# Feed-forward weights stored as they are and turned by the DMA that loads them, in a one-core attention and feed-forward block

## What is computed

```python
def block_qdq_weight(w, block=32, bits=4):
    wb = w.reshape(out_f, in_f // block, block)
    qmax = 2 ** (bits - 1) - 1
    scale = jnp.maximum(jnp.max(jnp.abs(wb), axis=-1, keepdims=True) / qmax, 1e-12)
    wq = jnp.clip(jnp.round(wb / scale), -qmax - 1, qmax) * scale
...
x = x + attention(layernorm(x), ctx, Wq, Wk, Wv, Wo)      # x: 8 x 128 x 512
h = act_qdq(layernorm(x))
up, gate = act_qdq(h @ wu.T), act_qdq(h @ wg.T)           # w_gate, w_up: 1376 x 512
gate = act_qdq(gate * fixed_qdq(sigmoid(gate)))
x = x + act_qdq(gate * up) @ wd.T                         # w_down: 512 x 1376
```

## Time and profile before

| | us |
|---|---|
| median of 3 runs | 944.35 |
| lowest, highest | 943.86, 945.84 |
| span of the profiled execution | 944.5 |
| attention groups, first L363 to the last project matmul | 110.6 to 695.6 |
| gate and up matmuls (L465) | 711.9 to 827.8 |
| last matmuls (L515) | 884.2 to 941.2 |

### The profile page before, as it was taken

How to read it: one execution, slowest core, us unless ns; L and a number is a source line. 1 busy time by engine, 2 the same in 40 slices (tenths; PEclk the granted TensorE clock), 3 DMA queues, 4 the chain that set the end, 5 groups by cost and what they waited for, 6 DMA issues and landing times. The chain is left out here.

```text
span 944.5 us, 16272 instructions
## 1 busy us (share of the span) xinstructions
PE 861.5 (91%) x5390; PEld 539.1 (57%) x5390; DVE 663.7 (70%) x1333; ACT 452.6 (48%) x1029; POOL 256.4 (27%) x382
## 2 busy tenths in 40 slices
PE   9999999999899999989999999999868999900898
PEld 3444777767577776657766677767533444400343
DVE  5754588886478888558888656667647459989741
ACT  5344455645346554436554454454513029868630
POOL 0000245453235464224455322222210002203000
PEclk9999999999989999999999999999998999965799
DMA  8013022222012313002232620000030000000001
GB/s 289 1 56 111 20 84 90 90 68 90 3 57 80 111 45 112 23 25 77 92 101 75 210 74 1 2 1 1 1 123 1 1 0 1 1 0 0 12 33 45
DMA packets 39756, 52.14 MB, mean 55 GB/s; under 512 B 2432, under 2 KB 18816, under 8 KB 39680
## 3 DMA queue, kind: packets, MB, share of 16 engines
q1 hardware_dynamic: 39680, 51.13, 16.7%
HBM read 40.37 MB, written 10.75 MB: 54 GB/s over the span
## 5 line engine op out<-in xcount | busy, mean ns | idle before, releaser
L523 ACT ACTIVATE arena<-bank 128x512 f16<-128x512 f32 (+1 forms) x329 | 189.5, 599 | 342.8 <-PE bank L363 234.9
L698 DVE SCALAR_TENSOR_TENSOR arena<-bank,arena 128x512 f16<-128x512 f32 (+1 forms) x329 | 219.1, 686 | 87.8 <-ACT arena L523 87.7
L270 PE MATMUL bank<-arena 128*128 128x256 f16 (+2 forms) x1872 | 261.8, 292 | 0.0
L270 PEld LDWEIGHTS bank<-arena 128*128 128x128 f16 (+1 forms) x1872 | 183.8, 98 | 69.0
L1067 POOL TENSOR_SCALAR arena<-arena,rsum 128x256 f32<-128x256 f32 x256 | 135.2, 528 | 241.2 <-DVE rsum L792 223.5
L465 PE MATMUL bank<-arena 128*128 128x512 f16 x528 | 116.3, 384 | 8.9 <-DVE arena L698 8.9
L387 PE MATMUL bank<-arena 128*128 (+1 forms) x512 | 121.0, 379 | 0.7 <-ACT arena L523 0.7
L579 ACT ACTIVATE arena<-bank,nmax 128x256 f32<-128x256 f32 x256 | 118.1, 487 | 6.2 <-DVE nmax L788 6.2
L784 DVE TENSOR_REDUCE nraw<-bank 128x2 f32<-128x512 f32 x128 | 85.4, 689 | 36.1 <-PE bank L352 36.1
L352 PE MATMUL bank<-arena 128*128 (+1 forms) x768 | 97.4, 277 | 9.4 <-issue 7.2
L352 PEld LDWEIGHTS bank<-arena 128*128 128x128 f16 x768 | 75.8, 99 | 33.6 <-issue 11.2
(11 more groups left out here) (91 smaller groups left out, 738.9 us busy)
## 6 DMA issues: line engine op xcount, KB each, us to landing
arena<-in_w_units SPq DMA_DIRECT2D x33, 256.0 KB, 2.8
w_ready<-arena SPq DMA_DIRECT2D x33, 256.0 KB, 2.1
arena<-w_ready SPq DMA_DIRECT2D x3, 2816.0 KB, 10.9
arena<-in_wq SPq DMA_DIRECT2D x32, 256.0 KB, 2.9
arena<-in_wo SPq DMA_DIRECT2D x32, 256.0 KB, 2.7
arena<-in_x SPq DMA_DIRECT2D x1, 2048.0 KB, 15.4
out<-arena SPq DMA_DIRECT2D x8, 256.0 KB, 2.0
arena<-in_wk SPq DMA_DIRECT2D x4, 256.0 KB, 5.2
```

The lines of the kernel that those rows point to most:

```text
L270: last = nc.tensor.matmul(bank, a(i, c), b(j, c), start=start and c == 0 and n == 0, stop=stop and c == chunks - 1 and n == 2)
L523: return nc.scalar.activation(dst, src, ACT.Copy, scale=scale)
L698: return nc.vector.scalar_tensor_tensor(out=dst, in0=src, scalar=scale, in1=part, op0=ALU.mult, op1=ALU.subtract)
```

## The change

PE's transposes of the weight units are gone, with their semaphore `w_mm`. ACT and DVE split a unit straight from `f_w`, so `w_ready` holds it untransposed. The slot of `f_w` is now free when `unit_lo` has read it (`w_lo`). SP's three loads become 33 transposing DMAs, one for each unit: 22 at the place of the first two, 11 at the place of the third.

```diff
             sp.wait_ge(pv_mm, 2 * QUADS + 1)
-            wgu_flat = wgu.rearrange("p u r n -> p u (r n)")
-            sp.dma_start(wgu_flat[:, 0:FT], ready_d[:, 0:FT]).then_inc(wg_loaded, 16)
-            sp.dma_start(wgu_flat[:, FT:2 * FT], ready_d[:, FT:2 * FT]).then_inc(wu_loaded, 16)
+            def load_turned(dst, u, loaded):
+                sp.dma_start_transpose(dst.rearrange("p r (c n) -> p (r c) n", n=P), w_ready[u]).then_inc(loaded, 16)
+            for u in range(FT):
+                load_turned(wgu[:, u], u, wg_loaded)
+            for u in range(FT, 2 * FT):
+                load_turned(wgu[:, u], u, wu_loaded)
             sp.wait_ge(wo_mm, NG * QUADS + 1)
-            sp.dma_start(wd_s.rearrange("p u r n -> p u (r n)"), ready_d[:, 2 * FT:UNITS]).then_inc(wd_loaded, 16)
+            for u in range(FT):
+                load_turned(wd_s[:, u], 2 * FT + u, wd_loaded)
...
-            def transpose_w(g, k):
-                v = g * FT + k
-                pe.wait_ge(w_dq, v + 2)
-                pe.wait_ge(w_lo, v + 1)
-                for c in range(HC):
-                    mm = nc.tensor.transpose(banks[WB][:, c * P:(c + 1) * P], f_w[:, k % 2, c * P:(c + 1) * P], ident[:, :])
-                mm.then_inc(w_mm, 1)
...
-                if not last(g) and 1 <= k <= FT:
-                    transpose_w(g, k - 1)
...
-            pe.wait_ge(wg_loaded, 16)
+            pe.wait_ge(wg_loaded, 16 * FT)
...
-                act.wait_ge(w_mm, v + 2)
+                act.wait_ge(w_dq, v + 2)
...
-                hi(f_out[:, k % 2, 0], banks[WB][:, :], W_SCALE).then_inc(w_hi, 1)
+                hi(f_out[:, k % 2, 0], f_w[:, k % 2], W_SCALE).then_inc(w_hi, 1)
...
-                lo(f_out[:, k % 2, 1], banks[WB][:, :], f_out[:, k % 2, 0], W_SCALE).then_inc(w_lo, 1)
+                lo(f_out[:, k % 2, 1], f_w[:, k % 2], f_out[:, k % 2, 0], W_SCALE).then_inc(w_lo, 1)
...
-                pool.wait_ge(w_mm, v + 1 if k == 0 else v)
+                pool.wait_ge(w_lo, v + 1 if k == 0 else v)
```

More of the change, by code:

```diff
@@ L161, in build @@
         q_mm, q_hi, q_lo = sem("q_mm"), sem("q_hi"), sem("q_lo")
-        amax_out, wscale_fl, wscale_out, w_norm, w_clip, w_round, w_dq, w_mm, w_hi, w_lo = (
-            sem(n) for n in ("amax_out", "wscale_fl", "wscale_out", "w_norm", "w_clip", "w_round", "w_dq", "w_mm", "w_hi", "w_lo"))
+        amax_out, wscale_fl, wscale_out, w_norm, w_clip, w_round, w_dq, w_hi, w_lo = (
+            sem(n) for n in ("amax_out", "wscale_fl", "wscale_out", "w_norm", "w_clip", "w_round", "w_dq", "w_hi", "w_lo"))
         ln2_stat, ln2_mv, ln2_var, ln2_rstd, ln2_out = (sem(n) for n in ("ln2_stat", "ln2_mv", "ln2_var", "ln2_rstd", "ln2_out"))
@@ L300, in _ @@
             keep_warm(8)
-            for s in (wo_mm, w_mm):
-                pe.sem_inc(s, 1)
+            pe.sem_inc(wo_mm, 1)
             pe.wait_ge(kv_free, NG)
@@ L493, in _ @@
             ffn_tiles(0, 1, 1, g_mm, g_free)
-            pe.wait_ge(wu_loaded, 16)
+            pe.wait_ge(wu_loaded, 16 * FT)
             for t in range(4):
@@ L503, in _ @@
             keep_warm(16)
-            pe.wait_ge(wd_loaded, 16)
+            pe.wait_ge(wd_loaded, 16 * FT)
             pe.wait_ge(u_free, 2 * FT + 3)
```

## The result

| | before | after |
|---|---|---|
| median (lowest to highest), us | 944.35 (942.13 to 945.84), 5 runs | 951.73 (950.29 to 954.43), 5 runs |
| ratio after to before, 95% interval | | 1.0077 [1.0051, 1.0104] |
| span of the profiled execution, us | 944.5 | 948.5 |
| start of the last attention step, us | 686.3 | 693.4 |
| first matmul of the feed-forward part | 711.9 | 716.3 |

The change makes the kernel 0.8% slower. The forecast was slower by 2.0 us; it is 7.4. The profiled execution of after is the fastest of its five: 950.29 with a span of 948.5, so 1.8 us lie around the span. With the same 1.8 us around it, that of before (944.5) would stand at 946.3 (an estimate), some 2 above its median here. That is why the spans are only 4.0 us apart.

What follows compares the result with a forecast made beforehand. PE sets the pace now, and DVE was to replace it at the same pace. A group -0.44 + 0.7 + 0.4 = +0.66, three groups +2.0: 946.5, median 0.15 lower, so 946.3 us; forecast 943 to 949.5, range 938 to 956.

Steps and rivals of the forecast that it cites:

- the hidden loads: 33 transposing loads before the feed-forward part: between 1.0 and 5.8 us a unit, both hidden, so no cost.
- the second rival: Attention steps: unit_lo and the last split both lose their turn to POOL in every step; 950 to 956 us, chance 0.15.
- steps 1: Step 1 of each group, where no split is due before: the full gain, -0.44 us a group.
- steps 2 to 8: Seven attention steps of each group: between 0 and +0.9 us, taken as +0.7 a group.
- steps 9 to 11: End of each group, where the next unit is late behind step 9's query weight splits: taken as +0.4 us a group.
- behind the attention: The program's tail, from 711.9 us on: no change.
- that late step: Second step of a pair: exponentials start late, unit_lo goes first (0.68 us), L1081 waits 0.5, last split precedes L1087 (0.92).
- The replay: Step 3 replayed from profile rows with turns between DVE and POOL, then a whole group: +0.66 us a group.
- The rival's price: Both splits losing every turn: another 0.4 us a step in seven steps and 0.4 behind them; +3.5 a group, +10.5 in all.
- the alternation of the forecast: Steps 2 to 9: two kinds in turn, some 8.7 and some 9.3 to 9.7 us; a pair 18.3, against 18.25 now.
- Rival 1: Attention: PE stays the bound, DVE fits, pairs take 17.4 to 17.9 us; 932 to 942 us, chance 0.21.

Runs made afterwards that it cites:

- The two halves of the change: Kernel before with only its three loads replaced by the transposing ones, 944.28 us; changed kernel with the three plain loads put back, 954.8 us.
- the moved operand: Changed kernel with unit_lo reading a PSUM bank instead of f_w: 930.22 us, ratio 0.9835.
- after_pool_late: Changed kernel with one tiny POOL multiplication added just ahead of unit_normalise (L1076): 947.77 us, ratio 1.0028.
- late_split: Changed kernel with the low part of unit k-2 split in step k, just ahead of the block scales, where POOL is idle: 927.48 us, ratio 0.9808.

## Why the prediction was right and wrong

**Right: the mechanism and the sign.** It said that DVE would take PE's place as the bound, by turns between a DVE instruction with two inputs in SBUF and a POOL instruction, and why the two must meet in each step. The two halves of the change, the moved operand and the moved instruction show this. Step 1 at 8.69 (-0.44), L1081 and `unit_lo` overlapping, 1.5 us for the `wo_s` split behind L1087 and the hidden loads came as written.

**Wrong: the size, by one step of the working.** The forecast was +2.0 (946.3), measured +7.4 (951.7). The forecast's own band, 943 to 949.5, does not hold that; the full range, 938 to 956, does, because it takes in the second rival's 950 to 956, which had a chance of 0.15. Term by term, for three groups:

| term | forecast | measured |
|---|---|---|
| steps 1 | -1.3 | -1.3 |
| steps 2 to 8 | +2.1 (+0.7 a group) | +7.8 (+2.6 a group) |
| steps 9 to 11 | +1.2 (+0.4 a group) | +2.5 |
| behind the attention | 0 | -2.7 in the profile |
| sum | +2.0 | +6.3, where the medians give +7.4 |

The step that failed is "In that late step ... the split goes first (0.68), L1081 waits 0.5, and the last split gets ahead of L1087 again". The replay had L1081 "not yet holding its turn, or just", took the first, and gave the other a place among the rivals with 0.15. The other is what happened: both splits lost in every step from 2 to 9, 1.56 and 1.50 us. The rival's price, 3.5 us a group or 10.5 in all, was near too: +3.0 a group, +9.1 in all, though its own terms (0.66, seven times 0.4, and 0.4) add up to 3.9. It named the right point, that L1081 starts before `unit_lo`, "by the 0.05 us that separate them"; measured 0.04. With the tie turned by the tiny instruction the alternation of the forecast appears, though at +1.5 a group and not +0.7, so the replay was short by some 0.8 a group even where its order held.

What decides this tie is ACT, not DVE's own order. This is read from the traces; no run moved ACT's part alone. In after, on ACT in step 2 (the first of the four exponentials, and the unit's high part, which `unit_lo` waits for):

```profile
128.34 0.47 ACT L574 ACTIVATE arena<-bank,nmax 128x256 f32<-128x256 f32 x1 [0.63 <-DVE nmax L783]
...
130.16 0.64 ACT L518 ACTIVATE arena<-arena 128x512 f16<-128x512 f32 x1
```

In each of steps 2 to 9 of after both engines set off from DVE's maxima (L783). In step 2 that is ACT with its exponentials at 128.34, DVE with its first softmax split at 128.35. On ACT's way the high part ends at 130.80 and `unit_lo` starts 0.03 us behind it (130.83), as in each of steps 1 to 9 of the trace. On DVE's way L799 ends at 130.71 and POOL starts 0.08 us behind it (130.79). The two ways are 2.49 and 2.44 us long, and `unit_lo` comes 0.03 to 0.04 us behind POOL in all of these steps. Step 10 shows what DVE does by itself. There it waits for a load, ACT's high part has been done for 1.9 us, and `unit_lo` comes first:

```profile
209.04 0.66 DVE L693 SCALAR_TENSOR_TENSOR arena<-arena 128x512 f16<-128x512 f32 x1
```

```profile
209.17 1.43 POOL L1076 TENSOR_TENSOR arena<-arena,winv 128x512 f32<-128x512 f32 x1 [1.93 <-DVE winv L799]
```

Could it have been read beforehand? Nearly. Step 3 of before has DVE's and POOL's rows of the two ways in the earlier trace rows, and on ACT:

```profile
139.89 0.48 ACT L579 ACTIVATE arena<-bank,nmax 128x256 f32<-128x256 f32 x1
```

From the first exponential to `unit_lo` that is 142.35 - 139.89 = 2.46 us, and from the first split to L1081 142.00 - 139.55 = 2.45. With the 0.02 us that the prediction itself gave the high part from SBUF, `unit_lo` comes 0.03 us second when both ways start together. That is too close to be sure of, but nothing in it speaks for `unit_lo` first, which the forecast took. The prediction weighed the tie as a chance of arrival, where two fixed chains set it alike in each late step. The Trainium skill, SBUF — State Buffer, section "Who interferes with whom", has the rule that issue order and not the kind of instruction decides who blocks. The runs agree (1.56 for DVE in after, 1.50 for POOL in `after_pool_late`); the prediction took the lock from that section and did not carry this second rule to its end.

**Steps 9 to 11.** Named was the chain through the query weight splits of step 9 and SP's load; step 10 came to 12.55, against 10.95, and the term was half as large as it should be. DVE in after, at the end of step 9 and in step 10, beside the earlier trace rows:

```profile
200.68 2.10 DVE L693 SCALAR_TENSOR_TENSOR arena<-arena 128x512 f16<-128x512 f32 x2
...
207.90 0.69 DVE L794 TENSOR_REDUCE amax<-arena 128x16 f32<-128x512 f32 x1 [1.93 <-DMA arena<-in_w_units]
```

The two splits end at 202.78, 1.22 us behind step 10's start (201.56); before they ended at 202.31, 0.15 behind it (202.16). The replay had the split before them 0.57 late, for one lost turn of `unit_lo`; it is late by both splits' turns, and 1.1 us reach the chain. L794 so starts 1.2 us later in its step (6.34 and 5.11 behind the first transpose), and L1076 takes 1.43 us for 1.05 behind `unit_lo`: together the 1.6 us that step 10 grew by.

**The baseline.** The prediction set a span of 944.5 against a median of 944.35 as if they measured the same. The runs of after show 1.8 us around the span, so the profiled execution of before stands for some 946.3, above all five of its runs in this comparison, though near the medians of the kernel before in the later rounds (945.8 to 946.4). The forecast hardly moves by this, since it is a difference; a comparison of the two spans alone would have shown 4.0 us for 7.4.

**Rival 1** (PE stays the bound, 932 to 942) fell for the change as made, and is right for `late_split`: pairs of 17.4.

## What to carry to other kernels

Work taken from the busiest engine is worth only what the next engine lets through: PE gave 0.44 us a step, and DVE held the steps at up to 9.85 us, 1.2 above what PE needs. When an operand moves from PSUM to SBUF, look at which DVE instructions then have both inputs in SBUF, and what POOL runs at that moment; a place a few instructions earlier, where POOL is idle, can be the whole difference (951.7 and 927.5 us here). If two engines set off from the same event and meet again, follow both chains to that point, the one through the third engine too. Where they end within some hundredths of a microsecond of each other, take neither order for granted, and price both: whichever it is comes out so each time.

## What the runs showed of the hardware

- A turn between DVE (both inputs in SBUF) and POOL is taken for the whole instruction and by who is first, and 0.04 us are enough: 1.56 and 1.05 us for DVE and POOL when POOL leads, 0.70 and 1.50 when DVE leads. When DVE loses it ends 0.53 to 0.55 us behind the end of POOL's instruction, wherever in that one it began (1.56, 1.50 and 1.37 us, and 0.92 behind an L1067 in before). With one input in PSUM there is no turn (1.29 us for two, POOL's 1.05 unchanged).
- A transposing DMA of a unit (1024 rows of 128 fp16 values, 256 KB) went out every 1.35 us on one queue in most cases, 194 GB/s by its 262144 bytes, and landed 3.8 us after its issue. Whether issuing or moving sets that pace is not shown: SP is in each issue for 1.31 us, and the packets fill 91% of the 16 DMA engines' time (704.7 to 711.6 us). The two figures quoted from the Trainium skill ahead of the result lie on both sides of this, as the prediction said: 261 GB/s by DMA: Bandwidth & Descriptors ("Latency and other measured facts") is 1.0 us, too fast, and eight times the 1309 ns of VectorE: DVE Perf Modes ("The three transpose paths") is 10.5 us, eight times too slow for blocks in a row.
- The first all-reduce on POOL starts 3 us later while a plain load of 2.8 MB runs (8.92 and 5.96 us of idle time), and 0.2 to 0.7 us later beside the transposing loads (6.20 to 6.70), whose packets took more of the 16 DMA engines' time in that stretch (91% against 79%).
